# A graph network's routed expert layers: routing logits summed over the edges first, in narrow columns, and gathers of rows issued ahead of scatters

## What is computed

```python
h = x @ W_in + b_in
for l in range(3):
    agg = segment_sum(h[src], dst) / deg
    logits = concatenate([h, agg]) @ router_W[l] + router_b[l]
    vals, idx = top_k(logits, 2)
    gates = softmax(vals)
    # 4 weak experts: one matrix; 4 strong experts: two matrices
    moe = sum over the two chosen experts of gate * expert(agg)
    h = h + sigmoid(h @ conf_W[l] + conf_b[l]) * moe
return h @ W_out + b_out
```

## Time and profile before

| | us |
|---|---|
| median of 3 runs | 3236.22 |
| lowest and highest | 3234.08, 3238.60 |
| the profiled execution | 3227.19 |
| its span, from first to last instruction | 3225.4 |
| TensorE busy in the span | 2705.8 (84%) |
| VectorE busy | 1950.1 (60%) |
| ScalarE busy | 855.9 (27%) |
| GpSimd busy | 557.2 (17%) |
| TensorE's clock over the span, granted | 0.923 |

### The profile page before, as it was taken

The page is one execution under the profiler, slowest core; times in us unless marked ns, Lnnn a source line. Parts: engine busy times, 40 slices in busy tenths (PEclk is TensorE's granted clock), DMA queues, the critical chain, the costliest instruction groups (busy, mean ns, idle before and its releaser), DMA issues. The chain is left out here.

```text
span 3225.4 us, 48657 instructions
## 1 busy us (share of the span) xinstructions
PE 2705.8 (84%) x17743; PEld 1697.5 (53%) x17743; DVE 1950.1 (60%) x4144; ACT 855.9 (27%) x1613; POOL 557.2 (17%) x561
## 2 busy tenths in 40 slices
PE   2888889999989999999888767777867777868787
PEld 1666555555444544445534456634446653437675
DVE  7999555557256777776645455565455565545553
ACT  3888521224120000000022222222222222213221
POOL 2000000000000000000002255502135530235540
PEclk8899999999999999999988889998879988889995
DMA  5454467774017455544230012250012233002223
GB/s 127 138 161 140 110 202 215 215 237 145 22 46 209 150 169 154 178 131 124 59 100 15 16 58 73 69 168 18 14 36 71 70 99 113 15 15 69 73 65 126
DMA packets 368148, 339.89 MB, mean 105 GB/s; under 512 B 51832, under 2 KB 336221, under 8 KB 365354
## 3 DMA queue, kind: packets, MB, share of 16 engines
q1 hardware_dynamic: 324244, 282.51, 28.8%
q0 software_dynamic: 23648, 51.54, 5.7%
q10 hardware_dynamic: 20022, 2.64, 0.6%
HBM read 211.09 MB, written 125.50 MB: 104 GB/s over the span
## 5 line engine op out<-in xcount | busy, mean ns | idle before, releaser
L1961 PE MATMUL psum<-r_wd,room_a 128*128 128x512 fp8e4 (+1 forms) x2600 | 569.4, 375 | 0.9 <-ACT r_ht L286 0.9
L1961 PEld LDWEIGHTS psum<-r_wd,room_a 128*128 128x128 f16 x2600 | 241.1, 97 | 296.7 <-ACT r_ht L286 1.1
L2600 DVE SCALAR_TENSOR_TENSOR m_edge_room<-psum,m_b,m_b1s 128x512 f32<-128x512 f32 x192 | 141.1, 749 | 301.8 <-PE psum L2821 247.2
L2821 PE MATMUL psum<-x_nodes,m_weights 128*128 128x256 f16 x2304 | 301.6, 293 | 0.0
L2839 PE MATMUL psum<-m_weights,room_a 128*128 x2304 | 267.2, 273 | 1.0 <-DVE room_a L2618 1.0
L2821 PEld LDWEIGHTS psum<-x_nodes,m_weights 128*128 x2304 | 239.4, 106 | 40.7
L2351 POOL DMA_INDIRECT slot_list<-m_b,m_at_list x150 | 149.6, 997 | 630.1 <-DVE m_at_list L2558 591.7
L2371 POOL DMA_INDIRECT y_rows<-room_a,m_b x192 | 190.8, 994 | 300.7 <-DVE room_a L2618 263.5
L2839 PEld LDWEIGHTS psum<-m_weights,room_a 128*128 128x128 f16 x2304 | 225.3, 98 | 28.1 <-issue 1.8
L2801 PE MATMUL psum<-m_ident,x_nodes 128*128 128x128 f16 x768 | 65.6, 234 | 174.9 <-DMA x_nodes<-agg_rows,m_b 174.9
L2360 POOL DMA_INDIRECT x_nodes<-agg_rows,m_b x192 | 197.9, 1031 | 67.9 <-issue 57.3
(11 more groups left out here) (383 smaller groups left out, 4311.5 us busy)
## 6 DMA issues: line engine op xcount, KB each, us to landing
r_wd<-packed_sym SPq DMA_DIRECT2D x120, 640.0 KB, 4.2
packed_counts<-strip SPq DMA_DIRECT2D x21, 1800.0 KB, 7.8
sym_blocks<-packed_counts SPq DMA_DIRECT2D x88, 384.0 KB, 5.0
packed_sym<-sym_blocks SPq DMA_DIRECT2D x84, 384.0 KB, 3.5
m_edge_room<-y_rows SPq DMA_DIRECT2D x36, 512.0 KB, 5.3
w_stage<-in_L_gnn_strong_W SPq DMA_DIRECT2D x12, 1024.0 KB, 6.8
m_weights<-in_L_gnn_strong_W SPq DMA_DIRECT2D x24, 512.0 KB, 9.3
agg_rows<-m_edge_room SPq DMA_DIRECT2D x72, 128.0 KB
```

What stands on the lines that cost most here:

```text
L1961: m = pe.matmul(bank[pair[b]][:, 0:2 * cw], h16[:, part, p0 + i, :], f_[:, 2 * b:2 * b + 2, :], start=(p0 + i == 0 and part == 0), stop=(p ...
L2600: vec.scalar_tensor_tensor(wide[:, fs, :], ps, k_hidden, b1s[:, bass.ds(col + 2 * h, 2)][:, :, None].to_broadcast([P, 2, PG]), ALU.mult, A ...
L2821: m = pe.matmul(o_, w_, x[:, y_, kb, :], start=(kb == 0 and part == 0 and y_ == 0), stop=(kb == KB - 1 and part == 1))
```

## The change

The router's product with the mean is a sum over edges of `h @ router_W[l][256:]`, eight columns in place of 256. The new kernel makes that product for each tile of `h` first. TensorE turns the tile of `h` (`turn`), multiplies it by 17 columns (`inputs`: eight for the node itself, one for the confidence, eight for the edges), ScalarE and VectorE write the last eight as two float16 halves of a scale of their own (`input_high`, `input_low`, 16 columns), and TensorE sums these over the edges for all 25 destinations (`input_sums`, 25 matmuls of 16 columns for each source tile, all in one bank). This stands where the first six destinations were summed. Then the logits of all tiles are made, chosen, ranked and placed in one chain (`choose`, `ranks`, `assign`, `gates`, once a layer), each instruction over 25 tiles at a time. The state that was carried between runs is gone.

The full sums (`edges`) come behind, one destination after another, with none under the combination. Each takes 50 matmuls of 256 columns, in which both halves are added up in the same columns of PSUM; ScalarE and VectorE write the mean's halves straight from there. Four banks take turns. TensorE's ranks stand after the second destination. GpSimd scatters 50 entries of the list in one sequence, and SyncE reads the list back ahead of the store of tile 20.

In the pages GpSimd issues the gathers of page j+4 ahead of the scatters of page j. The loads of the experts' rows come in groups of three tiles, not four. The router's weights lie in another order and come by three DMAs for each layer in place of two, with no zeros written; VectorE's fills of constants stand behind the first scale, and a second scale is worked out behind the first in each layer.

```diff
-    HEAD = 6
-    CUTS_R = [0, 1, 5, 9, 13, 17, 21, NT - 1, NT]
-    RUNS = [range(a, b) for a, b in zip(CUTS_R, CUTS_R[1:])]
...
+    YT = 3
+    YG = [slice(i, min(i + YT, NT)) for i in range(0, NT, YT)]
...
+    EB = 4
+    LIST_AT = 20
...
+                for k in range(NT):
+                    if k == LIST_AT:
+                        sp.wait_ge(list_out, 32 * NT * (l + 1))
+                        sp.dma_start(fld.rearrange("p s f -> p (s f)"), slot_lists[l].rearrange("(p s) f -> p (s f)", p=P)).then_inc(list_in, 16)
+                    r_ = rows_of(k)
                     sp.wait_ge(e_rows_low, l * NT + k + 1)
-                    sp.dma_start(agg_rows[l][i * P:i * P + r_, :], rows16[k % 4][0:r_, :]).then_inc(agg_out[k % 4], 16)
-                for k in range(2):
-                    sp.wait_ge(list_out[k], listed((l + 1) * len(RUNS) - 2 + k))
-                sp.dma_start(fld.rearrange("p s f -> p (s f)"), slot_lists[l].rearrange("(p s) f -> p (s f)", p=P)).then_inc(list_in, 16)
+                    sp.dma_start(agg_rows[l][k * P:k * P + r_, :], rows16[k % AR][0:r_, :]).then_inc(agg_out[k % AR], 16)
...
-                for c_ in range(len(RUNS)):
...
-                    for t in range(n_):
-                        for k in range(2):
-                            pool.indirect_dma_start(out=slot_lists[l], out_offset=bass.IndirectOffsetOnAxis(ap=at_list[0:r_, c_ % 2, k, t:t + 1], axis=0),
-                                                    in_=put[0:r_, k, i0 + t, :], in_offset=None).then_inc(list_out[c_ % 2], 16)
+                pool.wait_ge(e_slots, l + 1)
+                for i in range(NT):
+                    r_ = rows_of(i)
+                    for k in range(2):
+                        pool.indirect_dma_start(out=slot_lists[l], out_offset=bass.IndirectOffsetOnAxis(ap=at_list[0:r_, k, i:i + 1], axis=0),
+                                                in_=put[0:r_, k, i, :], in_offset=None).then_inc(list_out, 16)
...
                 for j in range(PAGES):
+                    gather(j + GR)
                     for s in range(SUB):
                         pool.wait_ge(p_y, (l * PAGES + j) * SUB + s + 1)
                         pool.indirect_dma_start(out=y_rows[l], out_offset=bass.IndirectOffsetOnAxis(ap=fld[:, j * SUB + s, 1:2], axis=0),
                                                 in_=ysb[j % 2][s], in_offset=None).then_inc(y_out[j % 2], 16)
-                    gather(j + GR)
...
+                    vec.tensor_tensor(us[:, 0:1], sc[:, 4:5], usum[:, NLAY * KB + l:NLAY * KB + l + 1], ALU.mult).then_inc(steps.handle, steps.up())
+                    settle()
+                    power_scale(us[:, 0:1], us[:, 1:2], us[:, 2:3], us[:, 3:4])
+                    mark["u_scale", l] = steps.n - 1
...
+                def input_low(i):
+                    n = l * NT + i
+                    vec.wait_ge(u_high, 2 * (n + 1))
+                    vec.scalar_tensor_tensor(u16[:, i, :, 1], bank[2 + i % 2][:, NE + 1:2 * NE + 1], us[:, 1:2], u16[:, i, :, 0], ALU.mult,
+                                             ALU.subtract).then_inc(u_low, 1)
...
+                def rows_low(k):
+                    n, r_ = l * NT + k, rows_of(k)
                     vec.wait_ge(e_rows_high, n + 1)
-                    vec.scalar_tensor_tensor(rows16[k % 4][0:r_, H:2 * H], agg[k % HEAD][0:r_, :], sc[0:r_, 1:2], rows16[k % 4][0:r_, 0:H],
+                    vec.scalar_tensor_tensor(rows16[k % AR][0:r_, H:2 * H], bank[k % EB][0:r_, 0:H], rvec[0:r_, k:k + 1], rows16[k % AR][0:r_, 0:H],
                                              ALU.mult, ALU.subtract).then_inc(e_rows_low, 1)
 
...
+                    dve_more_first()
+                for x_ in range(NT + 3):
+                    if l and x_ < NT:
+                        dve_first_choice(l, x_)
+                    if l and 0 <= x_ - 1 < NT:
+                        dve_second_choice(l, x_ - 1)
+                    if 0 <= x_ - 2 < NT:
+                        low(x_ - 2)
+                    if 0 <= x_ - 3:
+                        input_low(x_ - 3)
...
+                choose()
+                rows_low(0)
+                rows_low(1)
+                assign()
+                gates()
+                for k in range(2, NT):
+                    rows_low(k)
+                    if 3 <= k < 3 + NPC:
+                        split_low(k - 3)
...
+                def high(i):
+                    if l:
+                        act.wait_ge(c_both, (l - 1) * NT + i + 1)
+                    act.activation(h16(i)[:, 0:H], h2[:, i, :], ACT.Copy, scale=sc[:, 1:2]).then_inc(e_high, 1)
+
+                def turned(i):
+                    act.wait_ge(t_turned, l * NT + i + 1)
+                    act.activation(hT[i % 2], bank[i % 2][:, 0:KB * P].rearrange("p (k n) -> p k n", n=P), ACT.Copy).then_inc(t_kept, 1)
+
+                def input_high(i):
+                    act.activation(u16[:, i, :, 0], bank[2 + i % 2][:, NE + 1:2 * NE + 1], ACT.Copy, scale=us[:, 1:2]).then_inc(u_high, 1)
+
+                def input_own(i):
+                    act.wait_ge(u_made, l * NT + i + 1)
+                    act.activation(own[:, i, :], bank[2 + i % 2][:, 0:NE + 1], ACT.Copy).then_inc(u_high, 1)
+
+                def rows_high(k):
+                    n, r_ = l * NT + k, rows_of(k)
                     act.wait_ge(e_summed, n + 1)
-                    if n >= 2:
-                        act.wait_ge(e_mean, n - 1)
-                    act.activation(lows[k % 2][0:r_, :], bank[k % HEAD][0:r_, H:2 * H], ACT.Copy, scale=cvec[0:r_, i:i + 1]).then_inc(e_lows, 1)
-                    act.wait_ge(e_mean, n + 1)
-                    if k >= 4:
-                        act.wait_ge(agg_out[k % 4], agg_stores(l, k % 4, k - 3))
-                    act.activation(rows16[k % 4][0:r_, 0:H], agg[k % HEAD][0:r_, :], ACT.Copy, scale=sc[0:r_, 1:2]).then_inc(e_rows_high, 1)
-
...
+                for x_ in range(NT + 1):
+                    if x_ < NT:
+                        high(x_)
+                        turned(x_)
+                    if x_:
+                        input_own(x_ - 1)
+                        input_high(x_ - 1)
+                rows_high(0)
+                act.wait_ge(e_gap, l + 1)
+                act.activation(sm[:, 6:8, :], sm[:, 4:6, :], ACT.Exp).then_inc(e_exp, 1)
+                for k in range(1, NT):
+                    rows_high(k)
+                    if 3 <= k < 3 + NPC:
+                        split_high(k - 3)
...
+                def turn(i):
+                    n = l * NT + i
+                    if l:
+                        pe.wait_ge(c_both, (l - 1) * NT + i + 1)
+                    if n >= 2:
...
+                def inputs(i):
+                    n = l * NT + i
+                    pe.wait_ge(t_kept, n + 1)
+                    if n >= 2:
+                        pe.wait_ge(u_low, n - 1)
+                    if n == 0:
+                        pe.wait_ge(mrw_in, MRW_IN)
                     for kb in range(KB):
-                        m = pe.transpose(bank[6][:, (KB + kb) * P:(KB + kb) * P + r_], agg[t % HEAD][0:r_, kb * P:(kb + 1) * P], ident[0:r_, 0:r_])
...
+                def input_sums(i):
+                    pe.wait_ge(u_low, l * NT + i + 1)
+                    of = u16[:, i].rearrange("p e x -> p (e x)")
+                    for d in (0, NT - 1, *range(1, NT - 1)):
+                        r_ = rows_of(d)
+                        m = pe.matmul(SUMS[0:r_, d * 2 * NE:(d + 1) * 2 * NE], A[:, i, d * P:d * P + r_], of, start=(i == 0 and d == 0),
+                                      stop=(i == NT - 1 and d == NT - 2))
+                    if i == NT - 1:
+                        m.then_inc(u_summed, 1)
+
+                def edges(k):
+                    n, r_ = l * NT + k, rows_of(k)
+                    if k >= EB:
+                        pe.wait_ge(e_rows_low, n - EB + 1)
+                    for i in range(NT):
+                        if k == 0:
+                            pe.wait_ge(e_low, l * NT + i + 1)
+                        for x_ in range(2):
+                            m = pe.matmul(bank[k % EB][0:r_, 0:H], A[:, i, k * P:k * P + r_], h16(i)[:, x_ * H:(x_ + 1) * H],
+                                          start=(i == 0 and x_ == 0), stop=(i == NT - 1 and x_ == 1))
+                    m.then_inc(e_summed, 1)
+
+                def ranks():
...
+                    pe.matmul(RANKS[:, 0:NT * NE], below16[:], of, start=True, stop=False)
+                    for d in range(1, NT):
+                        pe.matmul(RANKS[:, d * NE:NT * NE], ones16[:], of[:, 0:(NT - d) * NE], start=False, stop=(d == NT - 1))
+                    for t in range(NT):
+                        m = pe.matmul(RANKS[:, NT * NE:(NT + 1) * NE], ones16[:], of[:, t * NE:(t + 1) * NE], start=(t == 0), stop=(t == NT - 1))
                     m.then_inc(e_ranked, 1)
...
```

(52 more changed lines are left out.)

457 lines of the change are left out of this document (154 added, 303 removed).

## The result

The changed kernel takes **3202.2 us** (median of 4 runs, 3199.8 to 3204.4), the kernel before beside it 3237.4 (4 runs): ratio 0.9892, 95% interval 0.9875 to 0.9909. It is 35 us (1.1%) faster, where 346 were forecast: clear of the noise, but less than the 2% from which a change counts as faster here. The profiled execution took 3202.39 us, with a span of 3200.3.

The account below looks back on a forecast made before the run. It took TensorE, never fully busy, as held up by page gathers, work between sums and each layer's end. Savings of 57.4 + 65.5 + 63.3 (layers), 158.5 (pages) and 1 (output), 345.7 us, gave 2890 us from 3236.2; range 2845 to 2975.

Parts of the forecast that it names:

- Edge sums: Full sums over edges: 25 tiles of 50 matmuls of 256 columns, 5.46 us a tile, 136.5 us a layer.
- Routing in one chain: Choice, ranks and placing once a layer, then 50 list scatters taking 65 us, hidden under the sums; ranks cost 2 us.
- Pages: Experts' 32 pages a layer: gathers ahead of scatters leave TensorE the bound at 5.69 us a page, 190 us; 158.5 saved.
- Inputs of layer 0: Narrow router sums before layer 0's edge sums: 25 tiles at 1.8 us, 45 us, plus 2.5 for the last chain.
- Layers 1 and 2, from the pages' end to the first edge sum: Combination with narrow sums: 9.1 us less 0.8 to start, 48 for the tiles, 3.2 for the last tile's chain.
- End of the sums: From a layer's last sum to its first turned page: 8.2 us instead of 26.
- Output: Final output stage: a smaller first load saves 1 us.
- The wait of the pages only moves: Rival, pages: GpSimd's issues set the pace; 2968 us at 6.5 a page, 3049 if gathers wait anyway; chance 0.12.
- Narrow matmuls paced by their weights: Rival, narrow sums: weight loads make an input tile 3.8 us, 95 a layer, giving 3034 us; chance 0.05.
- don't pipeline: Rival, narrow sums: at 0.27 us a matmul, a tile takes 7.8 us, giving 3334, slower than before; chance 0.03.
- Routing late: Rival, end of sums: a misread order makes routing late and brings back 54 us, giving 2944; chance 0.06.

Follow-up runs that it names:

- e16: Changed kernel with layer 0's list scatters paced, layer 1's followed by 50 iotas, layer 2's by 50 plain transfers with 512-column sums; starved: 3118.8 us, kernel before 3225.1.
- e17: Changed kernel with list scatters paced at some 3 a tile in all three layers; starved: 3018.4 us, ratio 0.9328 to the kernel before.
- e10: The kernel before, unedited, run for its trace in the unstarved condition: 3156.5 us.
- e7: The changed kernel, unedited, run again in the unstarved condition: 2881.6 us, ratio 0.914 to the kernel before.
- e4: Changed kernel with each page's gathers asked for behind its scatters again, as in the kernel before; unstarved: 2981.8 us.
- e1: Changed kernel with list scatters spread at about 3 a tile and the list loaded at tile 23, not 20; unstarved: 2883.2 us, kernel before 3158.4.

## Why the prediction was wrong

**The step that failed** is one that the prediction left unsaid between "Edge sums" (136.5 us a layer) and "Routing in one chain" (65 us of scatters, "hidden"): that what GpSimd issues beside TensorE costs TensorE nothing. It was costed at nothing, with the list's due time as the only thing to check. In the condition in which the kernel was timed, those 50 scatters in one run cost the stretch of sums 59 to 62 us a layer. That is shown by e16 and e17: with pauses between the scatters the stretches take 207 to 213 us instead of 266 to 275. The kernel before had its scatters in groups of eight at most; its trace held only the small delays of ScalarE told above, and TensorE had two gaps of 0.25 us (that of 6 to 7 us before the last ranks of a layer is in e10 as well).

The same unpriced step sits in "Pages", which put a page at TensorE's 5.69 us. There the starved condition costs the changed kernel 142 us. That it is again the indirect transfers, four in each page, is argued from the same marks (gaps of TensorE without a releaser, ScalarE late); no run took them away or gave them pauses, so for the pages the cause is not shown.

**The rest of the sum came close, in part by luck.** Where nothing is starved, the changed kernel takes 2881.6; forecast were 2890, and 2881.5 for an execution like the profiled one. Terms, forecast against e7:
- Inputs of layer 0: 47.5, counted from the parking's end (1615.3 before, ScalarE's first half at 1612.2 in e7); measured 51.7 (to 1664.0). A narrow matmul was priced right (25 with their switch 0.88 us, forecast 0.92), but two float32 matmuls of 17 columns take 0.72 us, not 0.35: a tile 2.06, not 1.8.
- Edge sums, layer 0: 136.5 + 2 + 3 = 141.5; measured 139.7 (1664.0 to 1803.7). A tile of 50 takes 5.46 us.
- Layers 1 and 2, from the pages' end to the first edge sum: 59.5; measured 64.0 (2000.1 to 2064.1).
- End of the sums: 8.2; measured 10.0, and 11.2 in layer 2.
- In all, a stretch of layer 0 from the parking's end 197.2, measured 201.5 (the table's 207.1 begins 5.6 us earlier); of layers 1 and 2 209.2, measured 215.0 and 214.3.
- Pages: 190; measured 186.4, all but the start at the bound of 5.69. The prediction added up wrongly here: 2.5 + 4.3 + 31 x 5.69 is 183.2, not 187, and with its 3 for waits 186.2. And the saving was 34.7, 32.1 and 31.2 us, not 54, 54 and 51: the kernel before is slower by 23 to 24 us a layer in the record's condition, and the earlier trace rows's 57 us of waiting are 41 in the same layer of e10. e4 gives the order's share by itself: with the gathers behind the scatters 218.2 us, 32 more than 186.4.
- Output: 1 us; measured 2 (80.1 to 78.1).

So the stretches of sums came out 15 us longer and the pages 11 us shorter than forecast, and the start 3 us earlier; that they cancel is luck. The saving is 271 us there, not 346: the forecast took the stretches of the kernel before as the record had them, with 76 us of starving in them, but put those of the changed kernel at bounds without any. It gave the time of the one condition and the saving of neither.

By the table, the 312 us between forecast and measurement are what the starved condition costs the changed kernel, 320, less 8 by which the unstarved time lies under the forecast.

**The rivals.** "The wait of the pages only moves" came nearest in the pages (233 us), but by another way: not GpSimd's four issues over 5.69 us (e7 does 5.69 with the same four), but gaps without a releaser on TensorE and late answers of ScalarE. In the starved pages ScalarE's copy (L2645) starts 1.0 us (median, up to 6.5) behind the last transpose, against 0.26 us unstarved. "Narrow matmuls paced by their weights" and "don't pipeline": out, 0.035 us each. Here the Trainium skill, TensorE: Matmul & The Clock Gate, section "LDWEIGHTS (loading the stationary operand)" (a load is its columns over 1.2 GHz), would have given 2.7 us for 25; the trace has 0.88. "Routing late": out, in e7 the last list scatter is over at 1751, in the 16th tile of 25.

**The clock** was at 2.4 GHz up to 1696, when TensorE had already had gaps for 4 us, and at 1.2 GHz from then to 1752, as the windows above show: it fell as a consequence of the gaps and didn't cause them.

## To carry to other kernels

A trace shows only runs of instructions that the kernel had, and a small delay in it can be a large one in a longer run: ScalarE's 0.4 to 1.1 us behind eight scatters became 47.6 us under fifty. When a change joins many small pieces of one engine's work into one long run beside the busiest engine, price that run from below and from above, even where no semaphore ties the two. In this kernel it paid to give GpSimd's indirect transfers pauses; e16's longest run was six, with a pause of 2.7 us behind it. Unstarved that cost nothing measurable, starved it took the kernel from 3185 to 3202 us down to 3018. And before explaining a miss, run the unedited kernel again beside its edits: four edits had looked like four cures.

## What the hardware showed that was not expected

- In one of two conditions, GpSimd's indirect transfers without a pause starve the others: ScalarE is 4 us late behind the fifth and then does nothing for 47 us, and from the eighth on TensorE falls from a matmul each 0.109 us to one each 1.4 and then 2.8 us, steps that are multiples of 0.70 us. It is over 6 to 8 us behind the last one. Plain transfers (0.53 us each, 50 in a row) and iotas behind them don't prolong it. In the pages, with four indirect transfers each, the condition costs 44 to 50 us a layer, which none of the runs removed; pauses as in e17's sums (50 scatters in 95 us, 1.9 each) would by my estimate hold a page to some 7.6 us, more than the 7.3 it takes starved.
- The condition was the same within a set of runs and changed between sets, on one and the same chip. A packet on the queue of the indirect transfers took 0.125 us on the mean on record and 0.124 in e1, so the transfers themselves are not slower.
- A late packet of instructions isn't what holds TensorE. The traces have a DMA queue "instruction" whose 16 KB packets come in the sums once for each 120 to 136 matmuls, starved or not, which is why I take it for TensorE's. On record one came at 1682.6 and the next at 1753.9, when TensorE had already been back at its full pace for 1.4 us; it took 0.96 us, where those in the sums of e7's layer 0 took 0.9 to 1.7.
- Left open: what switches the condition, and whether other work on the machine does; at what point the indirect transfers get in the other engines' way; and how long a run of scatters must be to stop TensorE.
